# Gated cross-attention and switch attention on one core: the first half's 128-row turns become half turns in two row tiles, and the order of all engines is laid out in four phases a batch

## The reference, cut to what matters

```python
x = x + tanh(g_xattn) * xattn(ctx, ctx, layernorm(x), mask)     # first half
x = x + tanh(g_ffn)   * switch_attention(layernorm(x))          # second half
# xattn:
qh, kh, vh = split(q @ wq + bq), split(k @ wk + bk), split(v @ wv + bv)
attn = softmax(qh @ kh.T / sqrt(16) + mask * -1e9)
out  = (attn @ vh).merge() @ wo + bo
```

## Time and profile before

| | |
|---|---|
| three runs, median (lowest, highest) | 1263.4 us (1262.7, 1263.97) |
| the profiled execution, first to last instruction | 1261.3 us |
| TensorE busy | 1210.2 us, 96% |
| VectorE, ScalarE, GpSimd busy | 867.9, 619.3, 548.6 us |
| mean DMA rate | 159 GB/s |

### The profile page before, as it was taken

How to read it: one execution, slowest core, us unless ns; L and a number is a source line. 1 busy time by engine, 2 the same in 40 slices (tenths; PEclk the granted TensorE clock), 3 DMA queues, 4 the chain that set the end, 5 groups by cost and what they waited for, 6 DMA issues and landing times. The chain is left out here.

```text
span 1261.3 us, 43567 instructions
## 1 busy us (share of the span) xinstructions
PE 1210.2 (96%) x17464; PEld 969.5 (77%) x17464; DVE 867.9 (69%) x2460; ACT 619.3 (49%) x1481; POOL 548.6 (43%) x821
## 2 busy tenths in 40 slices
PE   5699999999999999999789999999999999999996
PEld 4477777777777777777568888888888888888885
DVE  3577777777777777777566676676776766766653
ACT  3466666666666666665334433433433443444431
POOL 3477777777777776777411212212212212212111
PEclk9899999999999999999999999999999999999998
DMA  9999999888887887787035665665665665665663
GB/s 233 198 198 195 211 196 197 181 183 182 182 179 182 184 183 180 179 174 167 19 82 133 145 148 136 145 148 140 142 148 136 146 147 137 146 146 137 144 149 94
DMA packets 263016, 200.41 MB, mean 159 GB/s; under 512 B 195934, under 2 KB 243872, under 8 KB 258720
## 3 DMA queue, kind: packets, MB, share of 16 engines
q1 hardware_dynamic: 262816, 197.64, 69.3%
HBM read 125.49 MB, written 72.11 MB: 157 GB/s over the span
## 5 line engine op out<-in xcount | busy, mean ns | idle before, releaser
L899 POOL TENSOR_SCALAR shifted<-raw,neg_max 112x375 f32<-112x375 f32 x512 | 326.1, 646 | 165.6 <-DVE neg_max L781 121.9
L781 DVE CUSTOM_DVE_ANT_0 raw<-bank_s,maskb 112x375 f32<-112x375 f32 x512 | 266.4, 544 | 104.0 <-issue 88.5
L686 ACT ACTIVATE probsT<-bank_t 128x512 f32<-128x512 f32 (+3 forms) x512 | 189.2, 459 | 106.9 <-PE bank_t L460 106.9
L447 PE MATMUL bank_s<-K_stack,Q_stack 128*112 128x375 bf16 x512 | 151.0, 335 | 5.1 <-DVE neg_max L781 4.7
L1442 DVE TENSOR_REDUCE max<-bank_s 112x4 f32<-112x448 f32 x128 | 78.7, 615 | 78.0 <-PE bank_s L1200 78.0
L460 PEld LDWEIGHTS bank_t<-ident,shifted 48*128 48x128 f32 (+1 forms) x3072 | 105.6, 139 | 27.8 <-issue 24.4
L460 PE MATMUL bank_t<-ident,shifted 48*128 48x48 f32 (+1 forms) x3072 | 122.9, 226 | 0.0
L1531 POOL TENSOR_TENSOR mix_bd<-pm_te,tok 128x448 f32<-128x448 f32 x32 | 30.8, 962 | 205.5 <-DMA pm_te<-pm_dram 205.5
L203 POOL TENSOR_SCALAR var_eps<-moments 112x1 f32<-112x1 f32 x32 | 7.1, 223 | 238.5 <-DVE moments L199 238.3
L1152 PE MATMUL bank_ab<-xnT,wq2T 128*128 128x224 f32 x512 | 109.5, 357 | 0.8 <-ACT qT L1335 0.6
L1152 PE MATMUL bank_ab<-xnT,wk2T 128*128 128x224 f32 x512 | 109.7, 357 | 0.0
(11 more groups left out here) (147 smaller groups left out, 2213.4 us busy)
## 6 DMA issues: line engine op xcount, KB each, us to landing
K_stack<-k_dram SPq DMA_DIRECT2D x64, 562.5 KB, 7.7
k_dram<-k_parts SPq DMA_DIRECT2D x32, 562.5 KB, 4.5
att_dram<-att_q SPq DMA_DIRECT2D x31, 511.0 KB, 4.0
att_th<-att_dram SPq DMA_DIRECT2D x31, 511.0 KB, 4.4
v_dram<-mv SPq DMA_DIRECT2D x32, 455.0 KB, 6.1
v<-v_dram SPq DMA_DIRECT2D x32, 455.0 KB, 4.0
K_stack<-k_dram SPq DMA_DIRECT2D x32, 375.0 KB, 9.2
Q_stack<-q_dram SPq DMA_DIRECT2D x64, 168.0 KB, 9.2
```

What stands on the lines that cost most here:

```text
L447: nc.tensor.matmul(bank_s[h % 2][0:S, 0:S2], Q_stack[:, p, h, :], K_stack[:, p, h, :], start=True, stop=True).then_inc(scores_ready, 1)
L686: act.activation(probsT[:, g % 2, first_u:end, lo:hi], bank_t[0:KP, bank, column:column + (end - first_u) * (hi - lo)].rearrange("p (u q) ...
L781: dve.tensor_tensor_reduce(raw[:, g % 2, j, :], bank_s[h % 2][0:S, 0:S2], c.maskb[:, :], -1.0, -LEAST, ALU.add, ALU.min, neg_max[:, g % 2, ...
L899: pool.tensor_scalar(shifted[:, g % 2, j, 0:S2], raw[:, g % 2, j, :], -1.0, neg_max[:, g % 2, j:j + 1], ALU.mult, ALU.add).then_inc(shift_ ...
```

## The change

The turns of context, x, heads back and heads are each replaced by two half turns (`turn_halves`): rows 0 to 63 and rows 64 to 127 go through two row tiles, into the two banks of `bank_ab`. The tiles `xn` and `heads` grow to 128 rows with zeros in the tail, `outT` and `xnT` to 128 columns; `heads` and `wo` get an order of heads to fit. ScalarE's copies gather the two halves from the two banks. The half turns are put between `weigh` and `turn`. The bodies of all engines are written anew in four phases a batch: scores with untiled work among them, then a weighing, then half turns, then the turn of a group. Scores 0 to 3 of a batch move into the last phase of the body before; context and x are turned three batches ahead and not two, in one place. `exchange` stores Q's parts ahead of K's. The number of bytes moved is the same. Of the diff, the parts that matter:

```diff
             def exchange(b, p, i):
 
                 by_partition = lambda t: t.rearrange("a q (t p) n -> p (a q) t n", p=P)
-                sp.wait_ge(k_split, b + 1)
-                sp.dma_start(by_partition(k_dram[bass.ds(b, 1)]), k_parts[:, p, :, :, :]).then_inc(k_stored[p], 16)
                 sp.wait_ge(q_split, b + 1)
                 sp.dma_start(by_partition(q_dram[bass.ds(b, 1), 0:PARTS]), q_parts[:, :, :, :]).then_inc(q_stored[p], 16)
                 sp.dma_start(by_partition(q_dram[bass.ds(b, 1), PARTS:Q_COPIES]), q_parts[:, 0:Q_COPIES - PARTS, :, :]).then_inc(q_stored[p], 16)
-                if not (isinstance(b, int) and b < 2):
+                sp.wait_ge(k_split, b + 1)
+                sp.dma_start(by_partition(k_dram[bass.ds(b, 1)]), k_parts[:, p, :, :, :]).then_inc(k_stored[p], 16)
+                if b >= 2:
                     sp.wait_ge(scores_ready, H * (b - 1))
                 sp.wait_ge(k_stored[p], 16 * i + 16)
...
-            def transposes(b, i, p):
-
+            def turn_halves(columns, width, src, f):
+
+                for r in range(2):
+                    rows = slice(r * HALF, (r + 1) * HALF)
+                    last = nc.tensor.transpose(bank_ab[0:f.stop - f.start, r, columns:columns + width], src[rows, f], c.ident[rows, rows])
+                return last
+
+            def turn_ctx(b):
+                p, i = b % 2, b // 2
                 pe.wait_ge(ctx_loaded[p], 32 * i + 32)
-                start = isinstance(b, int) and b < 2
-                if not start:
+                if 0 < b < 3:
+                    pe.wait_ge(q_copied, (EC + 1) * b)
+                elif b >= 3:
                     pe.wait_ge(v_copied, 2 * (b - 1))
-                if not (start and b == 0):
-                    pe.wait_ge(q_copied, (EC + 1) * b)
+                if b > 3:
+                    pe.wait_ge(x_done, b - 3)
                 for e in range(EC):
                     for k in range(KC):
-                        last = nc.tensor.transpose(bank_ab[:, e, k * KP:(k + 1) * KP],
-                                                   ctx_in[:, p, k, e * P:(e + 1) * P], c.ident[0:KP, 0:KP])
+                        last = turn_halves((e * KC + k) * HALF, HALF, ctx_in[:, p, k, :], slice(e * P, (e + 1) * P))
                 last.then_inc(ctxT_ready, 1)
 
-            def keys(b, p, t):
+            def keys(b, t, bank):
                 if t == 0:
                     pe.wait_ge(ctxT_copied, b + 1)
+                    if b >= 2:
+                        pe.wait_ge(xt_copied, b + 1)
+                elif b >= 2:
+                    pe.wait_ge(k_copied, 2 * (EC * b + 1))
                 for e in range(EC):
-                    last = nc.tensor.matmul(bank_ab[:, t, 0:S2], c.wk[:, e, t * P:(t + 1) * P], ctxT[:, p, e, 0:S2],
+                    last = nc.tensor.matmul(bank_ab[:, bank, 0:S2], c.wk[:, e, t * P:(t + 1) * P], ctxT[:, b % 2, e, 0:S2],
                                             start=(e == 0), stop=(e == EC - 1))
...
                 pe.wait_ge(xn_done, b + 1)
                 for e in range(EC):
-                    last = nc.tensor.transpose(bank_ab[:, 0, e * S:(e + 1) * S], xn[:, e * P:(e + 1) * P], c.ident[0:S, 0:S])
+                    last = turn_halves(X_AT + e * HALF, HALF, xn, slice(e * P, (e + 1) * P))
...
                 pe.wait_ge(headsT_copied, b + 1)
                 for g in range(NG):
-                    last = nc.tensor.transpose(bank_ab[0:S, 0, g * P:(g + 1) * P], headsT[:, g * S:(g + 1) * S], c.ident[:, :])
+                    last = turn_halves(g * HALF, HALF, headsT, slice(g * S, (g + 1) * S))
                 last.then_inc(heads_ready, 1)
 
             def heads_turn(b):
                 pe.wait_ge(heads_done, b + 1)
-                flat_heads = heads[:, :, :].rearrange("s h d -> s (h d)")
+                flat_heads = heads[:, :, :, :].rearrange("s r h d -> s (r h d)")
                 for e in range(EC):
-                    last = nc.tensor.transpose(bank_ab[:, 1, e * S:(e + 1) * S], flat_heads[:, e * P:(e + 1) * P], c.ident[0:S, 0:S])
+                    last = turn_halves(e * HALF, HALF, flat_heads, slice(e * P, (e + 1) * P))
                 last.then_inc(outT_ready, 1)
...
+            def body(b):
+
+
+                p = b % 2
+                back = b > 0
+                S_ = lambda n, *hs: [scores(n, n % 2, n // 2, h, n == 0) for h in hs if n < B]
+
+                S_(b, 4, 5)
+                if b + 2 < B:
+                    keys(b + 2, 0, 0)
+                S_(b, 6)
+                if b + 2 < B:
+                    queries(b + 2)
+                elif b + 2 == B:
+                    open_gates(0)
+                S_(b, 7)
                 if back:
                     weigh(b - 1, 1 - p, NG - 1, False)
-                S_(5, 6)
-                if ahead:
-                    keys(b + 2, p, 1)
-                S_(7)
-                if last:
-                    pe.wait_ge(o.gates_copied, 1)
+                turn(b, 0, b == 0)
+
+                S_(b, 8, 9)
+                if b + 2 < B:
+                    keys(b + 2, 1, 0)
+                S_(b, 10, 11)
+                weigh(b, p, 0, b == 0)
                 if back:
-                    if ahead:
-                        pe.wait_ge(k_copied, 2 * (EC * (b + 2) + 1))
+                    if b + 2 < B:
+                        pe.wait_ge(k_copied, 2 * EC * (b + 3))
+                        pe.wait_ge(q_copied, (EC + 1) * (b + 3))
+                    else:
+                        pe.wait_ge(o.gates_copied, 1)
+                        pe.wait_ge(o.xt_copied, b + 3 - B)
                     heads_back(b - 1)
-                S_(8)
-                turn(b, 0, first)
-                if ahead:
-                    pe.wait_ge(k_copied, 2 * EC * (b + 3))
-                if back:
-                    heads_turn(b - 1)
-                S_(9)
-                if front:
+                turn(b, 1, False)
+
+                S_(b, 12, 13)
+                if b + 1 < B:
+                    if back:
+                        pe.wait_ge(heads_done, b)
+                    else:
+                        pe.wait_ge(k_copied, 2 * EC * (b + 3))
+                        pe.wait_ge(q_copied, (EC + 1) * (b + 3))
                     values(1 - p, 0)
                     values(1 - p, 1).then_inc(va_ready, 1)
-                S_(10)
-                weigh(b, p, 0, first)
-                turn(b, 1, False)
-                S_(11)
-                if ahead:
-                    pe.wait_ge(v_copied, 2 * b + 3)
-                    turn_x(b + 2)
+                S_(b, 14, 15)
+                weigh(b, p, 1, False)
+                if back:
+                    if b + 1 < B:
+                        pe.wait_ge(v_copied, 2 * b + 3)
+                    heads_turn(b - 1)
+                turn(b, 2, False)
+
+                S_(b + 1, 0, 1)
+                if b + 1 < B:
+                    if back:
+                        pe.wait_ge(outT_copied, b)
+                    values(1 - p, 2).then_inc(vb_ready, 1)
                 else:
-                    open_x(b + 2 - B)
-                S_(12)
+                    open_proj(0)
+                S_(b + 1, 2)
                 if back:
                     project(b - 1)
-                S_(13)
-                if ahead:
-                    queries(b + 2)
-                elif front:
-                    open_gates(b + 2 - B)
-                if front:
-                    if back:
-                        pe.wait_ge(x_done, b)
-                    values(1 - p, 2).then_inc(vb_ready, 1)
-                S_(14, 15)
-                turn(b, 2, False)
-                weigh(b, p, 1, False)
+                S_(b + 1, 3)
+                if b + 1 == B:
+                    open_proj(1)
+                weigh(b, p, 2, False)
+                if b + 3 < B:
+                    turn_ctx(b + 3)
+                    turn_x(b + 3)
+                elif b + 1 < B:
+                    open_x(b + 3 - B)
+                turn(b, 3, False)
...
-            def ctx_copy(b, p, start):
+            def ctx_copy(b):
                 act.wait_ge(ctxT_ready, b + 1)
-                if not start:
+                if b >= 2:
+                    act.wait_ge(xt_ready, b + 1)
                     act.wait_ge(vb_ready, b - 1)
-                act.activation(ctxT[:, p, :, :], bank_ab[:, :, 0:SK], ACT.Copy).then_inc(ctxT_copied, 1)
-
-            def key_copy(b, p, i, t):
+                act.activation(ctxT[:, b % 2, :, :].rearrange("p e (k r s) -> p r (e k) s", r=2, s=HALF),
+                               bank_ab[:, :, 0:X_AT].rearrange("p r (n s) -> p r n s", s=HALF), ACT.Copy).then_inc(ctxT_copied, 1)
...
+            def body(b):
+                back = b > 0
+                if back:
                     exps(b - 1, NG - 1, False)
+                if b + 2 < B:
+                    key_copy(b + 2, 0, 0)
+                    query_copy(b + 2)
+                elif b + 2 == B:
```

(73 more changed lines are left out.)

241 lines of the change are left out of this document (90 added, 151 removed).

## The result

| | kernel before | changed kernel |
|---|---|---|
| median (lowest, highest) | 1263.05 us (1261.64, 1263.97), 4 runs | 1349.76 us (1348.11, 1351.61), 4 runs |
| ratio | | 1.068 (1.066 to 1.070) |
| profiled execution | 1261.3 us | 1347.6 us |

The changed kernel is 86 us slower. The forecast said slower, by 8 us; the time lies far above its range.

What follows compares the result with a forecast made beforehand. TensorE was taken to pace the kernel, with DMA close behind. Eight early DMA cycles +10.6 us, 22 later batches -4.6 and about 2 at the end gave +8.0: median 1271.4 us, forecast 1265 to 1278, range 1257 to 1284.

Steps and rivals of the forecast that it cites:

- TensorE's work: TensorE's matmuls and turns in a batch: 18.06 us falls to 17.3 us if nothing waits.
- The waits on TensorE: New waits at `heads_back` (0.17 us), `values` (0.3) and `keys` (0.05): 0.52 us a batch, giving 17.85 us.
- that I put at 0.4 like the product: VectorE's subtraction in `split_rest`, ahead of the heads that `values` needs: priced at 0.4 us.
- the three waits together: `heads_back`, `values` and `keys` on TensorE: taken as 0.52 us, bounds 0 and 1.0 us.
- The exchange: K and Q through DRAM: storing K last was to let DMA pace eight early batches, +10.6 us.
- no DMA wait in the early batches: Profile sign of a wrong forecast; batches 2 to 9 were to wait for `K_stack` or `Q_stack`.
- the cycle: One early batch paced by the DMA queue: 17.1 us of work plus 2.4 is 19.5 us (19.1 to 19.9).
- the bare gap: DMA queue between K's store and K's loads, with nothing else queued: 2.4 us (2.0 to 2.75).
- Rival (c): DMA engines bind late batches too: 18.3 us a batch, 19.9 early; 1280 us, 1285 at worst; chance 0.17.
- The chain of 17.4 us against 17.1 available: K's store to the first score needing the stack: 16.4 to 17.4 us needed, said to just fit late batches.
- 2 us more: Work left behind the last batch's first score, a value block and a projection: about 2 us (0 to 3).

Runs made afterwards that it cites:

- e3: Changed kernel with VectorE's Q split end behind the reads of scores 12 and 13, and SyncE's x fetch ahead of the exchange: 1289.6 us, 1.011.
- e5: Changed kernel with GpSimd's `key_rest` moved between the shifts of heads 0,1 and 2,3 of the section's last block: 1320.4 us.
- e7: Changed kernel with GpSimd's `key_rest` issued as two instructions of 128x375 instead of one of 128x750: 1362.4 us.
- e6: e3 with the fetches of context and x, except the first of x, issued between K's store and K's loads: 1283.5 us, 1.008.
- e11: e4 with `split_rest` behind `key_third`, both behind the reads of heads 14 and 15, and the fetches behind both stores: 1292.5 us, 1.020.
- e4: e3 with K's store ahead of Q's: 1284.5 us, 1.0055.
- e9: e10 with the fetches of context and x between K's and Q's stores: 1294.6 us, 1.020.
- e10: e4 with VectorE's `key_third` ahead of the reads of heads 14 and 15 and `split_rest` behind them: 1291.7 us, 1.016.
- e8: The changed kernel itself, run again on another chip: 1348.5 us, 1.060.

## Why the prediction was wrong

**TensorE's work: right.** The 14 pairs of half turns cost 0.55 us (context and x, 8 pairs), 0.27 (heads back, 4) and 0.17 (heads turned, 2), 0.99 us where 0.91 were forecast, within the bound. TensorE's own pace is 17.9 us in e3, forecast 17.85, 18.06 before. So the change does what its form says, and is worth 0.15 us a batch. That the pace agrees so closely is in part luck: the 17.85 hold 0.3 us for the wait of the values, which e3's order doesn't have, and 0.05 where 0.28 was measured; the work alone, by these waits, is about 17.46 us (17.9 - 0.16 - 0.28, an estimate) and not 17.3.

**The waits on TensorE: the failed step.** In the changed kernel `heads_back` waits 0.16 us for K's copies, forecast 0.17. `keys` follows its scores by 0.65 instead of 0.37 us, a wait of 0.28 where 0.05 was forecast. `values` for `heads_done` was to wait 0.3 us, and waits 2.1. The term that failed is the subtraction "that I put at 0.4 like the product": 2.24 us. The price was good for the instruction alone. The rows for it in the kernel before (0.39) would have told the same. With 2.24 in its place the prediction's own sum gives 0.3 + 1.84 = 2.1 us, as measured. What the step left out was to ask what GpSimd does at that moment in the new order. The forecast bound of 1.0 us for the three waits together had no mechanism in it that could give 2.

This is what the Trainium skill states, page "SBUF — State Buffer", section "SBUF: two separate sides": VectorE and GpSimd share one pair of ports under an exclusive lock, which a VectorE instruction with two SBUF inputs needs against a GpSimd instruction that reads SBUF, and the one that comes second is blocked for the whole of the other. The traces agree in what collides (two SBUF inputs: 0.39 to 2.24 us; an input in PSUM: 0.42 and 0.54 us unchanged) and in the exclusive hold (ends 0.24 to 0.26 us after GpSimd in the changed kernel, e5 and e7). They go beyond it in one thing: in the changed kernel the subtraction was there 0.38 us ahead of `key_rest`, while GpSimd's shifts still ran, and was served after both. The 1.6 us that `key_rest` takes, added to the 0.3 of the prediction, would have had `values` 1.9 us late; that is an estimate by the page's rule.

**A wait not seen.** The prediction named neither `moments_of` nor x among the waits, and put batch 1 at 62.6 us with cycles of 19.5 from there on. Batch 1 began at 63.35 but lasted 31.85. The order of VectorE shows `moments_of(b + 3)`; the fetch that feeds it stands in SyncE's order, behind an exchange, and the two were not laid side by side.

**The exchange: the sum right, but covered, and not all of its reasoning.** The changed kernel itself shows none of the early DMA waits, since batches of 20 us leave the exchange mostly 1.7 to 4.6 us to spare; the sign "no DMA wait in the early batches" was named beforehand as one of being wrong. In e3 the cycle came out as forecast: 19.57 us for 19.5, +11 us for +10.6, with a DMA share of 0.90 over the eight (17.6 us of work for 17.1) and the bare gap of 2 us for 2.4. Rival (c) held in part too: for "The chain of 17.4 us against 17.1 available" the traces give 16.4 to 18.8, 17.3 on average, about half of e3's late batches wait for their stack, and they take 18.23 us, not 17.85. But a part of the reasoning fell: the gap isn't a hole that any transfer may fill (e6, e11). Only K's store first (e4) shortened the early cycle.

**What follows from a wait.** The forecast had no term for the clock. In the changed kernel the half-clock stretches come behind the waits for heads and cost 12 us of the 86, and some 1.4 more in batch 1. It isn't the heads that matter: in e3 three stretches come behind waits of 2.18, 2.26 and 1.72 us for the stack. e9 and e10, whose waits are 1.4 us at most, have none between 58 and 650 us. Not every wait of 2 us is followed by one, and what decides that is open.

**The rest.** Behind the first score of batch 31 the forecast had 2 us more, the values and a projection of the last batch, and 6.2 were measured. That stretch varies from run to run (660.0 us in e8, 662.1 here, the same kernel), and about 25 us of it are at half clock against about 14 in the kernel before. How much of the 6.2 us each of these makes isn't settled.

## What to carry to other kernels

Before an instruction of VectorE is moved, read what GpSimd runs at its new place: one with two SBUF inputs is held until GpSimd is through, and the row of its old duration says nothing of that. When a consumer is moved one batch ahead, find the fetch that feeds it on the queue's own order. And in a loop through DRAM don't count holes in the queues alone: here moving a fetch from one hole to another gained nothing, a store moved ahead of another did, and the engine that is to shorten the chain must have room at that place (e10).
